# Experts without a norm inside: routing two tiles ahead, in four parts of ranking

## What is computed

```python
def _L1_ffn_ref(x, gate_w, gate_b, W1, b1, W2, b2):       # hidden width 128
    logits = xf @ gate_w + gate_b
    probs = jax.nn.softmax(logits, axis=-1)
    top2_vals, top2_idx = jax.lax.top_k(probs, 2)
    cw = jnp.zeros((N, Ee), ...).at[jnp.arange(N)[:, None], top2_idx].add(top2_vals)
    # for every expert: out += cw[:, e] * (gelu(xf @ w1 + b1) @ w2 + b2)

def _L3_ffn_ref(x, Wr, br, ln_g, ln_b, W1, b1, W2, b2):   # hidden width 256
    # two best of the softmax, weights over the two; the experts see a second layer norm of x
```

## Time and profile before

| | us |
|---|---|
| median of three runs | 2224.24 |
| profiled execution, its time | 2236.28 |
| its span | 2234.5 |
| TensorE busy, share of the span | 1797.1, 80% |
| VectorE | 1068.6, 48% |
| ScalarE | 958.1, 43% |
| GpSimd | 431.2, 19% |
| mean granted TensorE clock | 0.89 |

### The profile page before, as it was taken

The page is one execution under the profiler, slowest core; times in us unless marked ns, Lnnn a source line. Parts: engine busy times, 40 slices in busy tenths (PEclk is TensorE's granted clock), DMA queues, the critical chain, the costliest instruction groups (busy, mean ns, idle before and its releaser), DMA issues. The chain is left out here.

```text
span 2234.5 us, 37728 instructions
## 1 busy us (share of the span) xinstructions
PE 1797.1 (80%) x14164; PEld 768.0 (34%) x14164; DVE 1068.6 (48%) x1723; ACT 958.1 (43%) x1127; POOL 431.2 (19%) x315
## 2 busy tenths in 40 slices
PE   5877999978996887665377775659999858599997
PEld 2542333333432332222355554223333323233332
DVE  1346667524553564288133332557666228434332
ACT  3124555544344343556233342535555530445553
POOL 0001222210000444000212211202232216212222
PEclk8698999989998898898578786979999979899999
DMA  4001331300002443034433334303313111033233
GB/s 139 10 10 39 76 74 40 77 19 19 1 0 53 99 115 77 0 136 188 113 109 97 95 91 160 148 5 73 76 39 76 39 19 19 18 88 83 63 92 76
DMA packets 67104, 153.78 MB, mean 69 GB/s; under 512 B 37448, under 2 KB 37448, under 8 KB 62240
## 3 DMA queue, kind: packets, MB, share of 16 engines
q1 hardware_dynamic: 66976, 151.97, 25.6%
HBM read 109.71 MB, written 29.64 MB: 62 GB/s over the span
## 5 line engine op out<-in xcount | busy, mean ns | idle before, releaser
L685 ACT ACTIVATE ARENA<-PS,W 128x1024 f32<-128x1024 f32 x448 | 474.6, 1109 | 332.4 <-PE PS L605 332.4
L536 POOL TENSOR_TENSOR ARENA<-ARENA 128x512 f32<-128x512 f32 x224 | 293.0, 1308 | 1239.4 <-DVE ARENA L820 1236.2
L605 PE MATMUL PS<-ARENA,W 64*128 64x512 f32 x1792 | 461.6, 635 | 1.0 <-ACT ARENA L685 1.0
L617 PE MATMUL PS<-ARENA,W 128*64 128x512 f32 x1792 | 434.8, 606 | 11.4 <-DVE ARENA L820 11.4
L820 DVE SCALAR_TENSOR_TENSOR ARENA<-PS,W,ARENA 128x512 f32<-128x512 f32 x256 | 190.5, 750 | 343.5 <-PE PS L617 278.8
L605 PEld LDWEIGHTS PS<-ARENA,W 64*128 64x128 f32 x1792 | 159.0, 192 | 262.2 <-issue 152.4
L617 PEld LDWEIGHTS PS<-ARENA,W 128*64 128x64 f32 x1792 | 109.1, 136 | 301.8 <-issue 208.2
L1197 DVE TENSOR_TENSOR ARENA<-ARENA 128x1024 f32<-128x1024 f32 x64 | 75.6, 1222 | 69.2 <-PE PS L1130 36.0
L1706 PE MATMUL PS<-ARENA 32*32 32x128 f32 x2048 | 83.4, 307 | 23.3 <-DVE ARENA L1641 23.0
L1167 ACT ACTIVATE ARENA<-PS 128x1024 f32<-128x1024 f32 x64 | 62.0, 1021 | 93.0 <-PE PS L1120 93.0
L1641 DVE TENSOR_TENSOR ARENA<-ARENA,PS 128x512 f32<-128x512 f32 x64 | 43.7, 684 | 112.8 <-ACT ARENA L1574 98.0
(11 more groups left out here) (215 smaller groups left out, 2182.6 us busy)
## 6 DMA issues: line engine op xcount, KB each, us to landing
ARENA<-scratch_g SPq DMA_DIRECT2D x64, 768.0 KB, 9.6
ARENA<-scratch_g SPq DMA_DIRECT2D x64, 256.0 KB, 4.0
ARENA<-XN SPq DMA_DIRECT2D x12, 512.0 KB, 3.3
ARENA<-XN SPq DMA_DIRECT2D x16, 256.0 KB, 2.3
scratch_x<-ARENA SPq DMA_DIRECT2D x8, 512.0 KB, 2.6
scratch_z<-ARENA SPq DMA_DIRECT2D x8, 512.0 KB, 3.2
scratch_b<-ARENA SPq DMA_DIRECT2D x8, 512.0 KB, 2.6
scratch_c<-ARENA SPq DMA_DIRECT2D x8, 512.0 KB, 2.6
```

Source lines behind the costliest of these rows:

```text
L536: nc.gpsimd.tensor_tensor(SUM[:, k, :], SUM[:, k, :], TMP[:, e % 2, :], ALU.add)\
L605: last = mm(PS[:, (b % 2) * R + r, :], w(layer + "_w1", b * 128, (b + 1) * 128, half(r)), XE[half(r), k, :], start=True, stop=True)
L617: last = mm(PS[half(r), 4 + e % 2, :], w(layer + "_w2", b * C, (b + 1) * C), H[:, b % 4, r * T:(r + 1) * T], start=part == 0, stop=part == ...
L685: f(H[:, b % 4, :], PS[:, (b % 2) * R:(b % 2) * R + R, :].rearrange("p a b -> p (a b)"), ACT.Gelu, bias=w(layer + "_b1", b, b + 1)).then_i ...
```

## The change

For the layers with norms=0, AHEAD is 2: in tile t, tile t + 2 is prepared. The router's tokens have two buffers of their own (XR) with semaphores of their own (e_router); SyncE loads them with routed(p). Before the first tile, the logits of tiles 0 and 1 are made into one PSUM bank, ranked and weighed as one batch of 16 groups (WIDE), and transposed and copied one after the other. The last two tiles prepare nothing. rank is cut into first and second and weigh into weigh and gate (the three last steps), and the places are new. The layers with norms keep their places.

```diff
@@ -448,19 +449,24 @@
...
+            AHEAD = 1 if norms else 2
+            XR = XS if norms else a.take(2, T)
+            ROUTES = NT - AHEAD + 1
...
+            def route(p):
+                return p if AHEAD == 1 else p - 1
...
+            WIDE = AHEAD * GR
...
@@ -469,25 +475,25 @@
...
+                dve_at = {-1: "keep", 0: "start 3", 1: "3 3 norm", 3: "first second", 4: "keep2 weigh gate start2 3",
                           5: "3 3 norm2"}
             elif norms == 1:
                 pe_at = {0: "center", 1: "vary", 4.5: "logits", 6.5: "turn"}
                 act_at = {0: "square", 5: "bend", 6.5: "rows"}
-                dve_at = {-1: "keep", 0: "start 3", 1: "3", 2: "3 norm", 4: "rank", 5: "weigh"}
+                dve_at = {-1: "keep", 0: "start 3", 1: "3", 2: "3 norm", 4: "first second", 5: "weigh gate"}
             else:
                 pe_at = {0: "logits", 2.5: "turn"}
                 act_at = {1: "bend", 2.5: "rows"}
-                dve_at = {1: "rank", 3: "weigh"}
+                dve_at = {0: "first", 1: "second", 3: "weigh", 4: "gate"}
                 if blocks == 2:
-                    pe_at = {1: "logits", 5.5: "turn"}
-                    act_at = {3: "bend", 5.5: "rows"}
-                    dve_at = {2: "rank", 4: "weigh"}
+                    pe_at = {1: "logits", 6.5: "turn"}
+                    act_at = {4: "bend", 6.5: "rows"}
+                    dve_at = {2: "first", 3: "second", 5: "weigh", 6: "gate"}
 
             assert router is None or a.used <= ROUTED.start
 
             def over(m):
...
@@ -511,18 +517,29 @@
...
+
+                    def routed(p):
+                        if p > 1:
+                            sp.wait_ge(g_logits.sem, g_logits.at(max(route(p - 2), 0) + 1))
+                        tokens = XN if router is None else router
+                        sp.dma_start(XR[:, p % 2, :], tokens[:, p * T:(p + 1) * T]).then_inc(e_router[p % 2].sem, 16)
+
+                    if norms:
+                        for p in range(NT):
+                            spread(p)
+                    else:
+                        routed(0)
+                        routed(1)
                         input_of(0)
                         input_of(1)
-                    spread(0)
-                    for t in range(NT - 1):
-                        if not norms and t + 2 < NT:
-                            input_of(t + 2)
-                        spread(t + 1)
+                        routed(2)
+                        spread(0)
+                        spread(1)
+                        for p in range(2, NT):
+                            if p + 1 < NT:
+                                routed(p + 1)
+                            input_of(p)
+                            spread(p)
...
@@ -560,25 +577,29 @@
...
-                            pe.wait_ge(e_input[k].sem, e_input[k].at((turn + 1) * INPUT))
-                            pe.wait_ge(g_rows.sem, g_rows.at(p))
-                        for g in range(G):
-                            last = mm(PS[:, SIDE, g * R * E:(g + 1) * R * E], XR[:, k, g * TOK:(g + 1) * TOK],
+                            pe.wait_ge(e_router[k].sem, e_router[k].at((turn + 1) * 16))
+                            if not col:
+                                pe.wait_ge(g_rows.sem, g_rows.at(p))
+                        for g in range(col, col + G):
+                            last = mm(PS[:, SIDE, g * R * E:(g + 1) * R * E], XR[:, k, (g - col) * TOK:(g - col + 1) * TOK],
                                       w(layer + "_wg"), start=True, stop=True)
...
+                        return last
...
+                    def transpose(p, k, col=0):
...
-                        pe.wait_ge(g_split.sem, g_split.at(p + 1))
+                        if col:
+                            pe.wait_ge(g_rows.sem, g_rows.at(p))
+                        elif norms or not isinstance(p, int):
+                            pe.wait_ge(g_split.sem, g_split.at(route(p) + 1))
                         for g in range(G):
-                            last = mm(PS[0:GW, SIDE, g * TOK:(g + 1) * TOK], GATES[:, g, :], w("ident"),
+                            last = mm(PS[0:GW, SIDE, g * TOK:(g + 1) * TOK], GATES[:, col + g, :], w("ident"),
...
@@ -606,7 +629,14 @@
...
-                    def tile_of(t, k, i, more=True):
+                    def tile_of(t, k, i, more=True, ahead=True):
+                        def side(at):
+                            if ahead:
...
+                                    prepare(pe_at.get(at), t + 1, 1 - k, i + k)
+                                else:
+                                    prepare(pe_at.get(at), t + 2, k, i + 1)
+
                         def down(b):
                             e, part = divmod(b, blocks)
                             if part == 0:
@@ -624,25 +654,33 @@
...
-                                up(t + 1, 1 - k, 0)
+                                up(t + 1, 1 - k, 0, i + k)
                                 up(t + 1, 1 - k, 1)
-                            if more:
-                                prepare(pe_at.get(n), t + 1, 1 - k, i + k)
+                            side(n)
                             down(2 * n)
                             down(2 * n + 1)
-                            if more:
-                                prepare(pe_at.get(n + 0.5), t + 1, 1 - k, i + k)
...
+                            side(n + 0.5)
...
+                    else:
+                        logits(0, 0, 0)
+                        logits(1, 1, 0, G).then_inc(g_logits.sem, 1)
+                        pe.wait_ge(e_input[0].sem, e_input[0].at(16))
+                        up(0, 0, 0)
+                        up(0, 0, 1)
+                        pe.wait_ge(g_split.sem, g_split.at(1))
+                        transpose(0, 0)
+                        transpose(1, 1, G)
...
-                    tile_of(NT - 2, 0, NT // 2 - 1)
-                    tile_of(NT - 1, 1, NT // 2 - 1, more=False)
+                    tile_of(NT - 2, 0, NT // 2 - 1, ahead=AHEAD == 1)
+                    tile_of(NT - 1, 1, NT // 2 - 1, more=False, ahead=False)
...
@@ -685,35 +725,42 @@
...
+                    def tile_of(t, k, more=True, ahead=True):
+                        def side(at):
+                            if ahead:
+                                prepare(act_at.get(at, ""), t + AHEAD, (k + AHEAD) % 2)
+
...
-                                prepare(act_at.get(n - 0.5, ""), t + 1, 1 - k)
+                            side(n - 0.5)
...
-                            if more:
-                                prepare(act_at.get(n, ""), t + 1, 1 - k)
...
+                            side(n)
...
+                    else:
+                        bend(1, WIDE)
+                        bend_up(0, 0)
+                        bend_up(0, 1)
+                        rows(0, 0, True)
+                        rows(1, 1, True)
...
@@ -740,34 +787,49 @@
...
+                    def best(chain, src, m, sel, SC, W1):
+                        step, rank_of = chain.step, w("rank").unsqueeze(1).to_broadcast([P, m.shape[1], E])
+                        step(v.tensor_reduce(m, src, AX.X, ALU.max))
+                        step(v.tensor_tensor(SC, src, over(m), ALU.is_equal))
+                        step(v.tensor_tensor(SC, SC, rank_of, ALU.mult))
+                        step(v.tensor_reduce(W1, SC, AX.X, ALU.max))
+                        step(v.tensor_tensor(sel, SC, over(W1), ALU.is_equal))
+
+                    def first(p, wide=GR):
+
+                        chain = Chain(dve, g_chain, route(p) * (RANK + WEIGH))
+                        EX, EY, D, L, M, SC, S1, S2, GATE, M1, M2, W1, W2 = narrow(wide)
+                        dve.wait_ge(g_logits.sem, g_logits.at(route(p) + 1))
+                        v.tensor_tensor(L, PS[:, SIDE, 0:wide * E].rearrange("p (a e) -> p a e", e=E),
+                                        w(layer + "_bg").unsqueeze(1).to_broadcast([P, wide, E]), ALU.add)\
+                            .then_inc(g_taken.sem, 1)
+                        dve.wait_ge(g_taken.sem, g_taken.at(route(p) + 1))
+                        best(chain, L, M1, S1, SC, W1)
+                        chain.step(v.scalar_tensor_tensor(M, S1, -3.0e38, L, ALU.mult, ALU.add))
+                        assert chain.n == FIRST_STEPS
+
+                    def second(p, wide=GR):
+                        chain = Chain(dve, g_chain, route(p) * (RANK + WEIGH) + FIRST_STEPS)
+                        EX, EY, D, L, M, SC, S1, S2, GATE, M1, M2, W1, W2 = narrow(wide)
+                        best(chain, M, M2, S2, SC, W1)
+                        if over_all:
+                            chain.step(v.tensor_tensor(EX[:, :, 0:E], L, over(M1), ALU.subtract))
+                        chain.step(v.tensor_tensor(D, M2, M1, ALU.subtract))
+                        assert chain.n == RANK - FIRST_STEPS
+                        dve.sem_inc(g_ranked.sem, 1)
...
@@ -780,10 +842,14 @@
 
```

(73 more changed lines are left out.)

82 lines of the change are left out of this document (27 added, 55 removed).

## The result

The changed kernel takes 2258.85 us (median of 4 runs, 2253.0 to 2260.87) against 2222.35 us before (4 runs). The ratio is 1.0164, with a 95% interval of 1.0116 to 1.0211: slower by 26 to 47 us. The profiled execution has a span of 2259.1 us.

What follows compares the result with a forecast made beforehand. Bound: TensorE's own work in L3; in L1 TensorE plus VectorE's logits-to-gates chain and clock falls. L3 +26.1 and L1 +5.4 gave +31.5 us on 2224.24, about 2256 us, range 2237 to 2270.

Steps and rivals of the forecast that it cites:

- The likeliest case: Whole kernel: L3 +26.1 and L1 +5.4 us, about 2256 us (2247 to 2264), chance 0.62.
- The gates behind a product (L3): L3's transposes: TensorE waits 2.83 us for gates after expert 6's product, in six tiles, 17.0 us.
- The clock in L3: L3 after each transpose wait: granted clock falls in five tiles of six, 8.0 us, bounds 0 and 10.
- rival 1: L3 and L1: stalls as forecast, but no added clock falls; L3 +18.1, total between 2238 and 2246, chance 0.16.
- L3's start and last-but-one tile: L3's ends: doubled start +3.1 us, last-but-one tile without logits and transposes -2.0.
- L1's tile: L1 per tile: gates later +1.9, DMA wait -0.4, low clock +0.3; together +1.8 on 21.97, +10.8 over six intervals.
- L1's start: L1 before its first tiles: joint logits and ranking of two tiles delay the down at 725.29 by 4.0 us.
- End: L1's last tiles: tile 6 -1.6, its third batch to tile 7's -6.7, from there to the fold's end -1.1 us.
- Routing two tiles ahead has nothing to gain in L3: L3: TensorE's own work fills the 32.3 us tile, so more distance gains nothing after the start.
- The value I gave the distance in L1: L1: the gate DMA wait goes, worth 0.4 us a tile.
- Rivals 2 and 4: Rival 2: L1's clock low twice as long, 2267, chance 0.10; rival 4: gates ready at the transposes, about 2194, 0.04.
- Rival 3: L3 and L1: no addition under the gates and no clock fall; 2225, no change, chance 0.08.

Runs made afterwards that it cites:

- L3's gates at 5: Changed kernel with L3's three gate steps moved to follow the weights after expert 5: 2234.0 us, 1.0074 of before; L3 273.5 us.
- one less: Changed kernel with GpSimd leaving out one addition per tile, after expert 4's product in L1 and 6's in L3: L1 196.3, L3 282.2 us.
- the old places with the distance: Changed kernel, two tiles ahead, with every step back at its old place: 2216.7 us, 0.9999 of before; L1 179.8, L3 271.8 us.
- an order in which the tile is 19.4: Changed kernel with steps at old places and L1's transposes after the tile's last downs: 2206.8 us, 0.9929 of before; L1 172.4 us.

## Why the prediction was right

Predicted were +31.5 us, 2256 us; measured +29.5 and +31.4 by the stages (491.5 less 461.9, 493.4 less 462.0), and medians of 2258.85 and 2222.35. The likeliest case came in, and in L3 by its mechanism. In L1 the wait came in too, but part of the sum is luck.

- The gates behind a product (L3): stall 2.83 predicted, 2.76 measured (2.59 once), 16.4 us of the predicted 17.0. The order of the steps came as laid out from the row of expert 4's weights: 0.22, then 1.33. That this is where the time goes is shown by the run with L3's gates at 5, and the share of the addition by the run with one less. The Trainium skill, "SBUF — State Buffer", section "SBUF: two separate sides", gives the ports to whichever instruction starts first. The trace agrees: the gate step that started ahead of the addition took 0.22 us, the one that started after it 1.33. The moment by which a step ahead delays the addition shows only where the two start together: the addition took 1.35 us there instead of 1.26.
- The clock in L3 was mis-sized: five falls of six taken from L1, three of six measured, twice (5 and 6 us instead of 8), so not "most" of the tiles. L3's +22.7 lies between the +26.1 of the forecast and the +18.1 of rival 1, which had no fall. The five of six was itself one profile's number; the two others had six and three.
- L3's start and last-but-one tile: +1.1 predicted; 22.7 less 16.4 and 5.0 leaves 1.3.
- L1's tile: 23.8 predicted, 24.0 measured; transposes 15.5 after the logits predicted, 15.6 measured; over the six intervals from tile 0 +10.8 measured, where +9.2 was due after tile 6's -1.6. Two misses offset each other in this agreement. The prediction gave the distance -7.8 us in L1 (start +4.0, end -9.4, DMA wait 6 x -0.4) and the new places +13.2; set against the one profile of the old places with the distance, they were worth -11.3 and +18.1. Nor do wait and clock add up as the sum had them: with the wait 1.1 us shorter the tile didn't shrink, where the prediction would have given +0.8 instead of +1.9.
- L1's start: 32.1 us from the table load to the third pair of downs, where it was 28.5: +3.6 of the predicted 4.0. End: 15.1 for tile 6 (15.2 predicted) and 8.05 from there (7.7 predicted).
- "Routing two tiles ahead has nothing to gain in L3": the old places with the distance gave 271.8 against 270.8.
- The value I gave the distance in L1 was too low. I priced it by the DMA wait of the kernel before, 0.4 us a tile. Beside the old places the tiles went from 21.97 to between 20.1 and 21.9, 20.7 on average, and it allows an order in which the tile is 19.4. The 0.4 us was what remained of one path next to another of nearly the same length: from the copy of the rows at 776.10 to the third product at 791.00 and on to the next copy at 797.37 are 21.3 us. The three profiles of the kernel before show the exchange: fewer falls of the clock, longer DMA waits, the same L1.
- Rivals 2 and 4 did not come in: the clock fell at half of L3's waits, L1 grew by 6.8 and not by 15 us, and no gates were ready at the transposes. Rival 3's missing addition exists only in the kernel with one less.

## What to carry to other kernels

When a chain of small steps is prepared ahead for another engine, count the slack at the place where that engine waits, not the distance in tiles: here tile t + 2 was being prepared, and TensorE still waited 2.8 us in it, because the last three steps stood behind a product that could start only where the wait began. Place the last step of the chain at least one batch ahead of its consumer, keep it from splitting two products that free two banks, and let the consumer come as late as the distance allows; in this kernel that order was worth 0.7% over before, and the wrong one cost 1.6%. Price a step behind a product with the other engine's addition beside it: here 1.33 us instead of 0.22.

## What the runs showed of the hardware

A VectorE step with two SBUF inputs that takes 0.22 us alone took 1.33 us when GpSimd's addition had started 0.01 us before it, 0.22 when the two started together, and 0.23 with the addition left out. In L3, six waits of 1.65 to 1.72 us never lowered the granted clock; of six waits of 2.6 to 2.8 us every other one did, in all three profiles that have them. In L1 before, where the wait is 2.46 us with a shorter one ahead of it, the clock fell in five, six and three stretches of six. With the changed places, waits of 4.40 and of 3.30 us gave tiles of 24.0 and 23.9 us, at a mean granted clock of 0.93 and 0.86: the shorter wait was followed by more work at 1.2 GHz. Why the tile kept its length wasn't tried further, and the second of the two is one profile.
